# Five raw fold buffers asked for in the first scan steps, with ScalarE's and VectorE's start-up reordered

## The reference, cut to what matters

```
u = silu(conv(in_proj_w @ ctx) + conv_b)              # 256 channels
x_dbl = x_proj_w @ u                                  # dt_lo, B, C
delta = softplus(dt_proj_w @ dt_lo + dt_proj_b)
A = -exp(A_log)                                       # 16 states a channel
state = state * exp(delta*A) + (delta*u) * B          # scan over tokens
y = sum_n(state * C) + D * u
x = x + y * silu(layernorm(x))
...
x = x + ffn0(layernorm(x)); x = x + attention(layernorm(x), ctx)
x = x + ffn1(layernorm(x))
```

## Time and profile before

| what | value |
|---|---|
| time, median of 3 runs | 715.69 us (714.43 to 716.24) |
| time of the profiled execution | 718.81 us |
| its span | 717.0 us |
| TensorE (PE) busy | 639.6 us, 89% |
| VectorE (DVE) busy | 493.0 us, 69% |
| ScalarE (ACT) busy | 391.5 us, 55% |
| GpSimd (POOL) busy | 276.8 us, 39% |
| moved by DMA | 98.85 MB, mean 138 GB/s |
| mean granted TensorE clock | 0.961 of full speed |

### The profile page before, as it was taken

How to read it: one execution, slowest core, us unless ns; L and a number is a source line. 1 busy time by engine, 2 the same in 40 slices (tenths; PEclk the granted TensorE clock), 3 DMA queues, 4 the chain that set the end, 5 groups by cost and what they waited for, 6 DMA issues and landing times.

```text
span 717.0 us, 10136 instructions
## 1 busy us (share of the span) xinstructions
PE 639.6 (89%) x3320; PEld 501.4 (70%) x3320; DVE 493.0 (69%) x1034; ACT 391.5 (55%) x798; POOL 276.8 (39%) x280
## 2 busy tenths in 40 slices
PE   6657678999989999999989999999889987979894
PEld 2355444555667888888778999998778976858783
DVE  5999989999866565455476676677687645543545
ACT  4776566454155545445477777777747762412221
POOL 1366510001244434445265565555337840042103
PEclk9699968999999999999999999999999999989998
DMA  5568944665545454554158233240001201355423
GB/s 187 157 195 280 323 168 143 202 203 178 154 138 148 119 164 118 164 160 141 59 188 283 74 109 113 74 145 34 30 30 67 96 16 59 118 169 155 154 81 118
DMA packets 58132, 98.85 MB, mean 138 GB/s; under 512 B 7000, under 2 KB 26976, under 8 KB 58080
## 3 DMA queue, kind: packets, MB, share of 16 engines
q1 hardware_dynamic: 56544, 94.00, 41.2%
q0 software_dynamic: 1536, 4.20, 1.9%
HBM read 78.51 MB, written 19.66 MB: 137 GB/s over the span
## 4 chain that ended last, share of the span: by engine, by line
PE 64%; DVE 17%; ACT 9%; issue 5%; DMA 2%; POOL 1%; another core or an unknown queue 1%; SPq 0%; DVEq 0%; POOLq 0%; ACTq 0%
PE bank L96 13%; PE bank L97 13%; PE bank L98 13%; PE bank L568 6%; PE bank L847 5%; DVE state L1375 3%; PE bank L579 3%; ACT probs L1215 3%; PE bank L782 2%; PE bank L487 2%; PE bank L868 2%; DVE scores L1727 1%; ACT bank L973 1%; PE bank L836 1%; DVE stats L1310 1%
## 5 line engine op out<-in xcount | busy, mean ns | idle before, releaser
L1864 POOL TENSOR_TENSOR w_lo<-w_raw,w_hi 128x768 fp32r<-128x768 f32 (+1 forms) x70 | 113.4, 1621 | 174.9 <-ACT w_hi L936 174.0
L96 PE MATMUL bank<-xt_hi,w_hi 128*128 128x512 f32 x224 | 89.9, 401 | 1.3 <-DVE hidden_lo L1292 1.3
L98 PE MATMUL bank<-xt_hi,w_lo 128*128 128x512 f32 x224 | 88.6, 396 | 0.0
L97 PE MATMUL bank<-xt_lo,w_hi 128*128 128x512 f32 x224 | 88.5, 395 | 0.0
L936 ACT ACTIVATE w_hi<-w_raw 128x768 fp32r<-128x768 f32 (+1 forms) x70 | 52.1, 744 | 55.2 <-PE bank L98 44.1
L1215 ACT ACTIVATE probs<-scores,row_min 128x256 f32<-128x256 f32 x128 | 63.9, 501 | 33.1 <-DVE row_min L1727 32.9
L1971 POOL TENSOR_TENSOR probs<-probs,row_scale 128x512 f32<-128x512 f32 x64 | 66.7, 1042 | 5.0
L1727 DVE CUSTOM_DVE_ANT_0 scores<-bank,mask_bias 128x256 f32<-128x256 f32 x128 | 48.7, 418 | 12.6 <-PE bank L98 12.6
L487 PEld LDWEIGHTS bank<-identity,read_out 128*128 128x128 f32 x272 | 35.5, 156 | 26.5 <-DVE read_out L1385 11.6
L1083 ACT ACTIVATE gated<-bank 128x512 f32<-128x512 f32 x52 | 31.1, 597 | 41.8 <-PE bank L568 30.0
L1292 DVE TENSOR_TENSOR hidden_lo<-bank,hidden_hi 128x512 fp32r<-128x512 f32 x40 | 27.6, 690 | 37.3 <-ACT hidden_hi L936 36.2
(11 more groups left out here) (222 smaller groups left out, 1648.4 us busy)
## 6 DMA issues: line engine op xcount, KB each, us to landing
w_raw<-in_ffn_w SPq DMA_DIRECT2D x38, 384.0 KB, 3.5
b_rows<-bc_scratch SPq DMA_DIRECT2D x32, 256.0 KB, 4.4
c_rows<-bc_scratch SPq DMA_DIRECT2D x32, 256.0 KB, 3.6
w_raw<-fold_scratch SPq DMA_DIRECT2D x32, 256.0 KB, 2.7
experts<-in_ffn_w SPq DMA_DIRECT2D x16, 384.0 KB, 4.0
route_bc<-route_scratch SPq DMA_DIRECT2D x31, 192.0 KB, 3.4
slots_scratch<-nothing SPq DMA_DIRECT2D x2, 2944.0 KB, 13.2
slots_in<-slots_scratch SPq DMA_DIRECT2D x22, 256.0 KB
```

Source lines behind the costliest of these rows:

```text
L96: e.matmul(out, w_hi, m_hi, start=first, stop=False)
L97: e.matmul(out, w_hi, m_lo, start=False, stop=False)
L98: return e.matmul(out, w_lo, m_hi, start=False, stop=last)
L1864: e.tensor_tensor(lo[:, 0:n], w_raw[(p - WHOLE) % RAW][:, 0:n], hi[:, 0:n].bitcast(F32), ALU.subtract).then_inc(sem("w_lo"), 1)
```

## The change

Four things are edited.

1. `fold_raw` gets five buffers instead of two. The three new ones lie where `xt_hi` and `xt_lo` are written later. `load_fold(g)` waits for the multiply of head g-5 instead of g-2. Loads 2, 3 and 4 are issued in scan steps 0, 1 and 2, behind the step's piece of ffn weights; loads 5, 6 and 7 stand where loads 2, 3 and 4 stood.
2. ScalarE loads the silu table first, makes the taps and silus, and takes A's exponential behind the second table load.
3. VectorE negates `decay` behind the second variance, and `z_shift` of half 1 stands behind the first drive.
4. VectorE's read of step 16 stands ahead of `normalise_x(2)`, and the drive of step 19 ahead of `find_eight(2)`.

Some semaphores are joined: `decay_neg` and `decay_bank_pad` become `decay_ready`, `decay_pad` counts on `consts`.

```diff
+FOLD_RAW = 5
...
+        top[0] = region_of["xt_hi0"]
+        fold_raw += [place(f"fold_raw{i}", [P, PIECE + WO_PIECE]) for i in range(2, FOLD_RAW)]
...
 def fold_turn(g):
-                raw = fold_raw[g % 2]
+                raw = fold_raw[g % FOLD_RAW]
...
 def scan_decay(h, n):
-                at.wait_ge("decay_neg", 1)
+                at.wait_ge("decay_ready", 2)
...
+            e.preload_act_table_set("silu_and_others")
             at.wait_ge("ld_small", 16)
-            e.activation(decay[:, :, :], a_log, ACT.Exp).then_inc(sem("a_exp"), 1)
-            e.preload_act_table_set("silu_and_others")
...
             e.preload_act_table_set("natural_log_exp_and_others")
+            e.activation(decay[:, :, :], a_log, ACT.Exp).then_inc(sem("a_exp"), 1)
             activate_delta(0)
...
-            for h in range(HALVES):
-                find_z_shift(h)
+            at.wait_ge("a_exp", 1)
+            e.tensor_scalar(decay[:, :, :], decay[:, :, :], -1.0, None, ALU.mult).then_inc(sem("decay_ready"), 1)
+            find_z_shift(0)
             make_delta_u(0)
             scan_drive(0, 0)
+            find_z_shift(1)
...
             scan_drive(1, 1)
+            scan_read(1, 0)
             normalise_x(2)
-            scan_read(1, 0)
             scan_state(1, 1)
...
             scan_read(1, 1)
+            scan_drive(1, 3)
             find_eight(2)
-            scan_drive(1, 3)
             weigh_eight(2)
...
 def load_fold(g):
-                at.wait_ge("fold", 2 * (g - 1))
+                at.wait_ge("fold", 2 * (g - FOLD_RAW + 1))
...
                 if n < SPLIT:
                     fetch(n)
+                if n + 2 < FOLD_RAW:
+                    load_fold(n + 2)
                 for g in range(KV_HEADS):
-                    if g >= 2 and fold_step.get(2 * g - 3, DS) + 1 == n:
+                    if g >= FOLD_RAW and fold_step[2 * (g - FOLD_RAW) + 1] + 1 == n:
                         load_fold(g)
```

More of the change, by code:

```diff
@@ L165, in build @@
         assert top[0] <= region_of["route_bc0"]
+        top[0] = region_of["xt_hi0"]
+        fold_raw += [place(f"fold_raw{i}", [P, PIECE + WO_PIECE]) for i in range(2, FOLD_RAW)]
+        assert top[0] <= region_of["xt_whole"]
         top[0] = region_of["route_bc0"]
@@ L668, in fold_multiply @@
             def fold_multiply(g):
-                raw, turned = fold_raw[g % 2], fold_t[g % 2]
+                raw, turned = fold_raw[g % FOLD_RAW], fold_t[g % 2]
                 at.wait_ge("fold_t", 2 * g + 2)
@@ L968, in scan_decay @@
                 else:
-                    at.wait_ge("decay_pad", 5)
+                    at.wait_ge("consts", 12)
                     at.wait_ge("state", i - 4)
@@ L1632, in _ @@
             find_variance(0)
-            at.wait_ge("a_exp", 1)
-            e.tensor_scalar(decay[:, :, :], decay[:, :, :], -1.0, None, ALU.mult).then_inc(sem("decay_neg"), 1)
             at.wait_ge("conv", 2 * HALVES)
             e.memset(banks[:, 2:6, :].rearrange("p k (b s) -> p (k b) s", b=HB)[:, :, 0:1],
-                     0.0).then_inc(sem("decay_bank_pad"), 1)
+                     0.0).then_inc(sem("decay_ready"), 1)
             at.wait_ge("ld_x1", 16)
@@ L1903, in _ @@
                 e.memset(decay_t[i][:, :, :].rearrange("p c (b s) -> p (c b) s", b=HB)[:, :, 0:1],
-                         0.0).then_inc(sem("decay_pad"), 1)
+                         0.0).then_inc(sem("consts"), 1)
             split_gates()
@@ L2044, in load_fold @@
             def load_fold(g):
-                at.wait_ge("fold", 2 * (g - 1))
-                load(fold_raw[g % 2][:, 0:PIECE], attn_proj_w[g], f"ld_fold{g % 2}")
-                load(fold_raw[g % 2][:, PIECE:], attn_out_w[g], f"ld_fold{g % 2}")
+                at.wait_ge("fold", 2 * (g - FOLD_RAW + 1))
+                load(fold_raw[g % FOLD_RAW][:, 0:PIECE], attn_proj_w[g], f"ld_fold{g % FOLD_RAW}")
+                load(fold_raw[g % FOLD_RAW][:, PIECE:], attn_out_w[g], f"ld_fold{g % FOLD_RAW}")
             def store_fold(g):
```

3 lines of the change are left out of this document (1 added, 2 removed).

## The result

The changed kernel took 713.54 us in the median of ten runs (711.51 to 715.68), the kernel before 716.46 in the ten runs beside them: a ratio of 0.9963, with a 95% interval of 0.9949 to 0.9977. The ratio is one of means (713.63 to 716.24); the medians lie a little further apart, 2.9. That is a gain of 2.65 us (1.65 to 3.65), where 2.6 was predicted. The terms of that sum did not all come out as forecast, as the experiments will show, and their agreement with the whole is partly luck.

A forecast was written before the change was run, and what follows sets the result against it. VectorE's scan chain bounds the start, TensorE sets the pace from 116.69 us; 1.75 + 2.2 - 0.8 - 0.55 = 2.6 us faster, from a median of 715.69 to 713.1, range 710.8 to 715.8.

The forecast's parts named there:

- the rule that L622 carries the end with it: Where TensorE starts to spread the routes (116.69 us): each microsecond earlier there brings the end forward by one.
- The exponential and z_shift, +1.75: Start-up: moving A's exponential and the second z_shift starts scan step 1 1.75 us earlier, between 1.07 and 2.25.
- They gain ScalarE's 1.07 and no more: Start-up: the second half's deltas, coming through ScalarE's queue, gain only the 1.07 us that ScalarE gains.
- That frees 1.3 us: Start-up: ScalarE's first conv tap comes at about 6.4 instead of 7.69 us, waiting for weights and TensorE's first product.
- And is over: Start-up: GpSimd's drive starts 2.2 us earlier and has ended before the second half's two products, formerly 2.09 beside it.
- The late fold loads, +2.2: Scan steps 9 to 14: three pairs of loads vanish, drive 16 stops waiting for b_rows, scan step 16 gains 2.2 us.
- Drive 13's loss: GpSimd's late drive at 74.87 stretches read 12 by 1.5 us; expected to stay, since two fold loads remain ahead.
- The early fold loads, -0.8: Scan steps 1 and 2: the fuller queue delays b_rows for drive 6, losing 0.8 us, ends 0 and 1.6.
- the estimate of no loss: Early fold loads: at about 358 GB/s the 3.15 MB is in by 47.2 us, nothing lost, sum 3.4.
- The order, -0.55: First normalisation: read 16 ahead of x_norm and drive 19 ahead of find_eight lose 0.55 us at L622.
- so rstd will wait for drive and read: First normalisation: GpSimd's rstd lasts until about 101.3, nearly 3 us, moving x_norm 1.1 us later.
- the wait only moves: Rival on fold loads: 1.6 lost early, only 1.1 gained late, 0.7 us faster in all, 715.0; chance 0.30.

The follow-up runs named there:

- r3: The kernel before with only the start-up changed (A's exponential behind the silus, z_shift of half 1 behind the first drive); ratio to before 0.9989.
- r5: The changed kernel with the three early fold loads asked for in scan steps 0, 4 and 5 instead of 0, 1 and 2; 708.6 us, ratio to before 0.9953.
- r8: The changed kernel with only read 16 put back behind x_norm, drive 19 staying ahead of find_eight; traced for one mechanism, no time given.
- r10: The changed kernel with VectorE's second-half delta and delta_u put behind scan 1 instead of ahead of it; ratio to before 0.9987.
- r2: The kernel before with only the five fold buffers and the early fold loads; ratio to before 0.9998.
- r11: The changed kernel with the edits of r5 and r10 together; 707.68 us, ratio to before 0.9939.

## Why the prediction was right, and where it was not

The time (713.1 predicted, 713.5 measured) holds, and so do the signs of the three larger terms and the rule that L622 carries the end with it. Two mechanisms inside, those of the start and of the order, did not. Term by term, with the means of all traces that bear on each:

- *The exponential and z_shift, +1.75.* Measured 2.0 in the pair and +1.4 in the mean, counted from TensorE's first product. The mechanism was divided wrongly. "They gain ScalarE's 1.07 and no more" failed in the pair: scan 1 was bound by VectorE and GpSimd's drive 2, and z_shift gave 1.05 by itself, with the exponential's 0.98 on top. In r3, r5 and r8 it was ScalarE's delta that bound scan 1, as the prediction had it, though for want of TensorE's clock. "That frees 1.3 us" was too much: the tap came at 6.80, not 6.4, since TensorE's first product ended later than the estimate, and with the weights early (4.87 and 5.16 instead of 6.15) the exponential's place gives 0.25 and 0.40. "And is over" failed as well: drive 2 starts when read 0 is done and so does delta, so both move together, and delta_u stays beside the drive unless delta comes late (r3, r5, r8) or is moved (r10).
- *The late fold loads, +2.2.* Exact in the pair (2.21) and 1.4 in the mean (5.07 against 3.64 for scans 15 to 16). The mechanism is right; the size was taken from one execution of a wait that varies from 0.35 to 2.2. Drive 13's loss was rightly left in; it shrank by 0.4 in the mean (5.42 to 5.02) and in the pair by 0.5.
- *The early fold loads, -0.8.* Mis-sized. Measured -1.24 in the pair and -1.55 in the mean of six. Only drive 6 had been priced; the b_rows of drive 5, which stand behind a fold load as well, come late too. The rate was underrated (350 GB/s over 12 us, near the 358 that the Trainium skill, DMA: Bandwidth & Descriptors, Specifications, gives), and still the estimate of no loss made from that figure was wrong: with the engines 0.98 busy b_rows landed in 6.3 us, with 0.81 (r5) in 4.3.
- *The order, -0.55.* Measured +0.4. The failed step is "so rstd will wait for drive and read". The row it was read from, w_lo beside a drive and a read the earlier trace rows, is of a different, longer GpSimd step; that rstd takes 1.92 beside a drive was seen, and nothing said that a second step would lengthen it again. It took 1.92, not nearly 3.
- *Sum.* 1.4 - 1.55 + 0.4 + 1.4 + 0.4 = 2.05 (start, early loads, order, late loads, drive 13), inside the 1.65 to 3.65 measured; the pair of traces has 2.0 - 1.24 + 0.4 + 2.2 + 0.5 = 3.9 of its 4.5 at L622, and the rest is mostly the clock at the router products. The five buffers, taken alone, are nearly a wash: 1.4 + 0.4 - 1.55 = 0.25, and r2 measured 0.1. Against these means the predicted 2.6 had 0.8 too much for the late loads, 0.75 too little cost for the early ones and 0.35 too much for the start; the wrong sign of the order (0.95) and drive 13 (0.4) made up for more than half of that. So the agreement of 2.6 with 2.65 is luck, and the means stay 0.6 below the measured gain, within its interval.
- Of the rivals, "the wait only moves" described the folds best (1.6 lost at the early loads, only part of the 2.2 gained at the late ones), and the other parts then made up for it.

## What to carry to other kernels

A load asked for early is not free where small, timed loads stand behind it in the same queue: price every timed load behind it, not the last one alone, and keep lumps apart (three steps between two groups left one drive late by 0.5 us, where changing their order with one b_rows only moved a wait of 2.1 to 3.0). A gain upstream of a full queue is lost at the queue, as r10 showed and r11 undid, so mend the queue first. Before a term is made from one wait, look how much it varies: here the same wait was 1.59, 3.03 and 3.62 in three executions.

## What was not expected of the hardware

- VectorE's delta_u pair (128x512, both operands in SBUF) took 1.28 us alone and 2.56 beside GpSimd's drive, and neither the drive (2.36) nor a scan beside it (2.28, one operand in PSUM) was longer than usual. The drive is not always spared: beside read 15 of the kernel before it took 3.14.
- GpSimd's small power step took 1.01 alone, 1.92 beside one VectorE drive and 1.92 beside a drive with a read right behind; the read kept its 1.22.
- ScalarE's wait for the small weights ended at 6.15, 4.87 and 5.16 us in three executions of the same start, and TensorE's first product started at 4.09 to 4.87 in the fourteen profiled ones.
